# Order of work on ScalarE and VectorE in a fused four-stage kernel: when a partial sum is read, and when a masked copy is made

## Chip, cores and metric

The kernel runs on one core of a Trainium2 chip. The metric is the device time of one execution in microseconds, of which the median over several executions is given. A core has TensorE (PE, in the rows split into PE for matmuls and PEld for weight loads), VectorE (DVE), ScalarE (ACT), GpSimd (POOL) and SyncE (SP). ScalarE and SyncE also issue the DMAs of this kernel (ACTq and SPq in the rows).

## What is computed

The input x has the shape [128, 64, 1024] (batch, channel, time). Four residual stages follow one another, each over the whole tensor:

```python
x = x + L0(x, W[cond])              # per batch entry: a 64x64 mix of the channels
x = x + L1(x, K1, D1, length1)      # causal convolution along time with a kernel of 1024 taps per channel,
                                    # y * mask(t < length1)
x = x + L2(x, W2, bias, lora)       # x @ W2.T + bias + scale[adapter] * (x @ A.T) @ B.T along time
x = x + L3(x, K3, D3, length3)      # as L1, with the input masked too: y(u*mask) * mask
```

The taps are K = 2 Re(sum over n of C' exp(A dt l)). The last three stages treat each channel by itself: the convolutions mix times within a channel, and L2 has its 1024x1024 matrix along time.

## The kernel before

**Order of the whole.** First comes stage 0 (L0), with the weights and the tables of the taps prepared beside it, up to some 256 us of the span. After it a loop `body(g)` runs over 16 groups of four channels (HG = 4, NG = 16). `body(0)` is written out by itself (`early`), 1 to 13 are a hardware loop on ScalarE and VectorE, 14 has no group after the next (`more2` false), and 15 has no next group (`more1` false). Each engine has its own instruction order, written out by hand, and the engines meet at semaphores only. A pass over one group from 1 to 14 takes some 83 us.

**Precision.** Every operand of a matmul is split into two fp16 tiles, a high part (ScalarE rounds) and a low part (VectorE subtracts), and three products are summed. So ScalarE has `..._hi` helpers and VectorE `..._lo` helpers, and each low part waits for its high part.

**Stage 2 on TensorE** (`stage2`, lines 867 to 967). The 1024x1024 product is done by block products in the manner of Strassen's scheme with fewer multiplications. It is a sequence of 14 blocks, counted by `s2_summed`; here they are called block 1 to block 14. A block is 24 matmuls of line 899, and those with a low-rank part have 6 more of line 908. Blocks 1 and 2 fill the two SUM banks (PSUM 4 and 6); 3 and 4 the MIX banks (5 and 2); 5 and 6 the OWN banks (0 and 1); 7 and 8 add to the SUM banks; 9 and 10 add to the SUM banks again; 11 and 12 add to the MIX banks; 13 and 14 finish the SUM banks. Between two additions to a bank ScalarE must have copied out what stood in it at that moment, because that state is itself one of the wanted sums. This is `read_part` (line 1314; the activation is line 1320): it waits for the block (`s2_summed`), may issue a weight load (`load_w`, line 1308), reads the bank in two instructions into a tile `x3part`, and raises `s2_read`. TensorE waits for `s2_read` before the next block on that bank (line 950 for blocks 9 and 10):

```python
pe.wait_ge(s2_read, NREAD * g + 5 + p)                       # line 950, ahead of blocks 9 (p=0) and 10 (p=1)
block(SUM_AT[p], p, streamed(4), t_parts[2], False, False)
```

**The output of stage 2.** `add_part(n)` on VectorE (line 1890, instruction line 1894) adds a finished bank to its `x3part` tile once the block is done, and raises `s2_out`. `split_hi3(n)` on ScalarE (line 1327, instruction line 1333) waits for that and rounds the tile to fp16; `lo3(n)` on VectorE (instruction line 1898) makes the low part. In the same stretch the loaded channels of the next group are split: `x1_split_hi(g+1, h)` on ScalarE (line 1240, instruction line 1247) and `x1_split_lo(g+1, h)` on VectorE (instruction line 1793), four times each, in the order h = 2, 3, 0, 1. Blocks 13 and 14 wait for `s2_out` 3 and 4 (line 963), that is for `add_part(2)` and `add_part(3)`.

**Weights.** Some blocks take their weights from SBUF for good, the others from three slots that `load_w` fills from DRAM on the ACT queue. `load_w(5)` is issued in the third pair's `read_part(g, 0, ...)` and serves block 10, `load_w(6)` in `read_part(g, 1, ...)` serves block 11, and `load_w(7)`, after block 9, serves block 12.

**The end of a pass.** After stage 2 TensorE runs the states and convolution 1 of the next group (`states`, `near1`, `far1`) between those of convolution 3 of this group (`near3`, instruction line 987, and `far3`, line 1000). VectorE takes convolution 1 over into x by `take_conv1(g+1, h)`, a predicated copy under the mask (line 1795, instruction line 1800), which raises `c1_out`. `near3(g, 0)` waits for the third such copy and `near3(g, 1)` for the fourth (line 979, with `conv1_sums_read`). After a copy ScalarE rounds (`x2_split_hi`, instruction line 1251) and VectorE makes the low part (`x2_split_lo`, instruction line 1805).

**The past of convolution 3.** Where t is at or past the length, the output is the unchanged x. For this SyncE turns the split x by DMA transposes (`turn_x3`, instruction line 518), ScalarE scales the high part back (`past_half`, instruction line 1344), and VectorE adds the low part (`past_sum`, line 1844, instruction line 1848) and raises `past_ready`. SyncE waits for `past_ready` of rows 0 and 1 before it loads a table (line 473) and turns rows 2 and 3, since there are only two buffers. `take_row` (instruction line 1855) puts the past under the mask into the output.

**GpSimd** makes the tables of the taps (`make_tables`, lines 602 to 632) twice in a pass, and VectorE slows down while it runs.

Of the kernel before, what the change touches and what calls it, by code (L numbers as in the profile page):

```python
# [75 lines left out]
def build(nc, x, ids0, len1, ids2, len3, w0, ssm1, ssm3, w2, bias2, lora_a, lora_b, lora_s, out):  # L76
    with ExitStack() as ctx:
# [250 lines left out]
        SUM_AT, MIX_AT, OWN_AT = (4, 6), (5, 2), (0, 1)  # L328
# [32 lines left out]
        X1_ORDER = (2, 3, 0, 1)  # L361
# [718 lines left out]
        def _(act):  # L1080
# [159 lines left out]
            def x1_split_hi(g, h):  # L1240
                if isinstance(g, int) and g == 0:
                    act.wait_ge(x1_kept, NBLK)
                    act.wait_ge(x1_kept_last, 1)
                else:
                    act.wait_ge(x1_loaded[h], 32 * g)
                    at_least(act, out_stored[h // 2], 16 * (g - 1))
                nc.scalar.activation(x1_parts(g)[0][:, h], x1f[:, h], ACT.Copy, scale=XS / FS).then_inc(x1_hi, 1)  # L1247
# [66 lines left out]
            def read_part(g, p, bank, n_sum, row, slot, load=None):  # L1314
                act.wait_ge(s2_summed, NSUM * g + n_sum + p + 1)
                if load is not None:
                    load_w(load)
                for n in range(2):
                    o = row + 2 * p + n
                    e = nc.scalar.activation(x3part[slot + p][:, n * HW:(n + 1) * HW], ps[:, bank, n * HW:(n + 1) * HW], ACT.Identity,  # L1320
                                             bias=biasx[:, o:o + 1], scale=XS / FS)
                e.then_inc(s2_read, 1)
# [4 lines left out]
            def split_hi3(g, n, h0, row, slot):  # L1327

                if n < 6:
                    act.wait_ge(s2_out, NOUT * g + n + 1)  # L1330
                else:
                    act.wait_ge(s2_read, NREAD * g + n + 1)
                nc.scalar.activation(x3_quarter(x3h, h0, row), x3part[slot].rearrange("p (k h b) -> p k h b", k=2, h=2),  # L1333
                                     ACT.Copy).then_inc(x3_hi, 1)
# [28 lines left out]
            def body(g, more1, more2):  # L1363
                early = isinstance(g, int) and g == 0
                if more1 and not early:
                    bases_hi(0, g + 1)
                    table_hi(0, g + 1)
                act.wait_ge(low_scaled, g + 1)
                nc.scalar.activation(lowh.rearrange("p (h b) -> p h b", h=HG), lowf, ACT.Copy).then_inc(low_hi, 1)
                for h in range(HG):  # L1370
                    at_least(act, x3_turned[h], 32 * g)
                at_least(act, x3_lo, NBLK * g)
                if more1 and not early:
                    act.wait_ge(u_lo, made(0, g + 1) + 1)
                for p in range(2):
                    read_part(g, p, SUM_AT[p], 0, 0, 0)
                at_least(act, past_ready, HG * g)
                read_part(g, 0, MIX_AT[0], 2, NQ, 2, 3)
                read_part(g, 1, MIX_AT[1], 2, NQ, 2, 4)
                if early:  # L1380
                    store_tab(NBLK - 1, 1)
                act.wait_ge(low_diff, g + 1)
                nc.scalar.activation(lowdh, lowf.rearrange("p h b -> p (h b)")[:, 0:HW], ACT.Copy).then_inc(lowd_hi, 1)
                if more1:
                    for h in X1_ORDER[0:2]:
                        x1_split_hi(g + 1, h)
                if early:
                    act.wait_ge(tab_stored[1], 16 * NBLK // 2)
                split_hi3(g, 0, 0, 0, 0)
                if more1:  # L1390
                    for h in X1_ORDER[2:4]:
                        x1_split_hi(g + 1, h)
                read_part(g, 0, SUM_AT[0], 6, 0, 4, 5)
                split_hi3(g, 1, 0, 2, 1)
                read_part(g, 1, SUM_AT[1], 6, 0, 4, 6)
                if early:
                    scale_k(NBLK - 1, 3)
                    bases_hi(0, 1)
                    table_hi(0, 1)
                act.wait_ge(s2_summed, NSUM * g + 9)  # L1400
                load_w(7)
                split_hi3(g, 2, 2, NQ, 2)
                if early:
                    store_k(NBLK - 1)
                act.wait_ge(s2_summed, NSUM * g + 10)
                if more1:
                    load_w(2)
                split_hi3(g, 3, 2, NQ + 2, 3)
                act.wait_ge(s2_summed, NSUM * g + 11)
                if more1:  # L1410
                    load_w(0)
                split_hi3(g, 4, 2, 0, 4)
                bases_hi(1, g)
                act.wait_ge(s2_summed, NSUM * g + 12)
                if more1:
                    load_w(1)
                split_hi3(g, 5, 2, 2, 5)
                read_part(g, 0, 4, 12, NQ, 0)
                split_hi3(g, 6, 0, NQ, 0)
                read_part(g, 1, 6, 12, NQ, 0)  # L1420
                split_hi3(g, 7, 0, NQ + 2, 1)
                if not more1:
                    table_hi(1, g)
                if more1:
                    state_hi(0, g + 1, 0)
                    table_hi(1, g)
                    state_hi(0, g + 1, 1)
                    state_hi(1, g, 0)
                    state_hi(0, g + 1, 2)
                    state_hi(1, g, 1)  # L1430
                    past_half(g, 0)
                    state_hi(1, g, 2)
                    past_half(g, 1)
                    for h in range(HG):
                        x2_split_hi(g + 1, h)
                else:
                    for k in range(NCH - 1):
                        state_hi(1, g, k)
                for n in range(HG):
                    h = out_row(g, n)  # L1440
                    act.wait_ge(c3_summed, HG * g + n + 1)
                    at_least(act, out_stored[h], 16 * g)
                    nc.scalar.activation(outt[:, h].rearrange("p (m c) -> p m c", m=NCH),
                                         ps[:, 2 * (n % 2):2 * (n % 2) + 2, :].rearrange("p n (q c) -> p (n q) c", q=2)[:, :, ::-1],
                                         ACT.Copy, scale=1.0 / FS).then_inc(c3_out, 1)
                    if more2 and n == 1:
                        act.wait_ge(v_made, 2 * made(0, g + 2) + 2)
                    if more1 and n in (1, 2):
                        t_split_hi(g + 1, n - 1)
                        past_half(g, n + 1)  # L1450
                if more1:
                    for n in range(2, 4):
                        t_split_hi(g + 1, n)
# [11 lines left out]
        def _(dve):  # L1465
# [337 lines left out]
            def x2_split_lo(g, h):  # L1803
                dve.wait_ge(x2_hi, HG * g + h + 1)
                stt(x2l[:, h], x1f[:, h], XS / FS, x2h[:, h], ALU.mult, ALU.subtract).then_inc(x2_lo, 1)  # L1805
# [38 lines left out]
            def past_sum(g, h):  # L1844

                dve.wait_ge(past_hi, HG * g + h + 1)
                past_row = past[:, h % 2].rearrange("p (k t) -> p k t", k=NBLK)
                stt(past_row, x3t[:, h % 2, 1], 1.0 / XS, past_row, ALU.mult, ALU.add).then_inc(past_ready, 1)  # L1848
# [15 lines left out]
            def body(g, more1, more2):  # L1864

                early = isinstance(g, int) and g == 0
# [64 lines left out]
                if more1:  # L1931
                    state_lo(0, g + 1, 0)
                    table_lo(1, g)
                    state_lo(0, g + 1, 1)
                    state_lo(1, g, 0)
                    state_lo(0, g + 1, 2)
                    state_lo(1, g, 1)
                    take_conv1(g + 1, 0)
                    state_lo(1, g, 2)
                    take_conv1(g + 1, 1)  # L1940
                    past_sum(g, 0)
                    x2_split_lo(g + 1, 0)
                    take_conv1(g + 1, 2)
                    past_sum(g, 1)
                    x2_split_lo(g + 1, 1)
                    take_conv1(g + 1, 3)
                    x2_split_lo(g + 1, 2)
                    x2_split_lo(g + 1, 3)
                    t_rows(g + 1)
                else:  # L1950
                    for k in range(NCH - 1):
                        state_lo(1, g, k)
# [51 lines left out]
```

## Time and profile before

| What | Value |
|---|---|
| median of 3 runs | 1604.87 us (1602.5 to 1608.54) |
| the profiled execution, its own time | 1609.9 us |
| its span, first to last instruction | 1608.1 us |
| mean granted TensorE clock | 0.978 |
| TensorE matmul busy | 1508.5 us, 94% |
| VectorE busy | 1246.4 us, 78% |
| ScalarE busy | 743.8 us, 46% |
| GpSimd busy | 546.5 us, 34% |

The profiled execution lies 5.0 us above the median of the runs. A row of the timeline reads: start in us, duration in us, engine, line, operation, output<-inputs, shape, count; in brackets the idle time of the engine just before and what ended it. Matmuls overlap: one of 256 columns is shown with 273 ns, while the next starts 109 ns after it, so the distance of two starts tells more than a duration.

### The profile page before, as it was taken

The numbers are of one execution on the slowest core, as the hardware profiler recorded it, in microseconds if no ns is written. First come the engines' busy times: TensorE is split into PE (matmuls) and PEld (weight loads), VectorE is DVE, ScalarE is ACT, GpSimd is POOL, SyncE is SP. The second block draws the span as 40 slices with busy tenths as digits, with TensorE's granted clock in tenths as the row PEclk, the third lists the DMA queues.
The fourth block names the chain that finished last, engine by engine and source line by source line (L and its number), as shares of the span: only waits on it lengthen the run. The fifth ranks groups of instructions, "written<-read, shape, count | busy, mean of one in ns | idle before, by whom it ended". The sixth has DMA issues, their size and how long they took to land.

```text
span 1608.1 us, 36825 instructions
## 1 busy us (share of the span) xinstructions
PE 1508.5 (94%) x14983; PEld 1305.9 (81%) x14983; DVE 1246.4 (78%) x1525; ACT 743.8 (46%) x1084; POOL 546.5 (34%) x260
## 2 busy tenths in 40 slices
PE   7787776989999999999999999999999999999998
PEld 6677775778888888888888888888888888888887
DVE  7878786979595969696878787887878686969563
ACT  4444443435454535354545454545444454545443
POOL 2111103473333333333333334343434343434030
PEclk9889889999999999999999999999999999999999
DMA  7799996558575765658574757483848484857432
GB/s 225 259 323 377 339 370 223 131 119 196 131 187 139 172 153 153 173 129 192 126 191 121 193 119 204 107 219 89 225 95 214 90 229 96 223 104 210 111 132 67
DMA packets 455255, 287.63 MB, mean 179 GB/s; under 512 B 331528, under 2 KB 410896, under 8 KB 453072
## 3 DMA queue, kind: packets, MB, share of 16 engines
q1 hardware_dynamic: 405904, 174.57, 46.5%
q10 hardware_dynamic: 49216, 110.98, 19.8%
q8 instruction: 119, 1.95, 0.5%
q14 instruction: 16, 0.13, 0.0%
HBM read 161.30 MB, written 75.96 MB: 148 GB/s over the span
## 4 chain that ended last, share of the span: by engine, by line
PE 66%; DVE 19%; DMA 6%; issue 5%; ACT 3%; ACTq 0%; SPq 0%; DVEq 0%
PE ps L899 27%; PE ps L803 8%; PE ps L987 6%; DMA arena<-in_x_dram 5%; PE ps L876 5%; PE ps L908 4%; PE ps L847 4%; PE ps L751 3%; DVE arena L1793 3%; PE ps L1000 3%; PE ps L813 3%; DVE arena L1848 3%; DVE arena L1805 2%; DVE lowd L1885 2%; PE ps L687 1%
## 5 line engine op out<-in xcount | busy, mean ns | idle before, releaser
L899 PE MATMUL ps<-arena,w2t 128*128 128x256 f16 x4608 | 525.4, 273 | 17.2 <-ACT arena L1320 14.0
L899 PEld LDWEIGHTS ps<-arena,w2t 128*128 128x128 f16 x4608 | 450.1, 98 | 77.5 <-issue 17.6
L618 POOL TENSOR_TENSOR arena<-arena 128x1024 f32<-128x1024 f32 x31 | 78.3, 2525 | 796.7 <-DVE arena L1855 430.2
L1898 DVE TENSOR_TENSOR arena<-arena 128x512 f16<-128x512 f32 x128 | 104.3, 815 | 126.0 <-ACT arena L1333 126.0
L1333 ACT ACTIVATE arena<-arena 128x512 f16<-128x512 f32 x128 | 80.6, 630 | 253.7 <-DVE arena L1894 252.7
L751 PE MATMUL ps<-arena 128*128 128x128 f32 x1024 | 147.7, 309 | 51.5 <-DMA arena<-in_x_dram 26.4
L751 PEld LDWEIGHTS ps<-arena 128*128 128x128 f32 x1024 | 139.7, 221 | 57.0 <-DMA arena<-in_x_dram 28.1
L1320 ACT ACTIVATE arena<-ps,biasx 128x256 f32<-128x256 f32 x256 | 103.3, 470 | 85.5 <-PE ps L908 51.3
L847 PE MATMUL ps<-arena 128*128 128x512 f16 (+1 forms) x768 | 136.9, 329 | 5.6 <-DVE arena L1793 5.6
L987 PE MATMUL ps<-arena 128*128 128x256 f16 (+1 forms) x1536 | 137.1, 246 | 2.6 <-DVE gbuf L1800 2.6
L987 PEld LDWEIGHTS ps<-arena 128*128 128x128 f16 x1536 | 122.0, 98 | 16.5 <-DVE gbuf L1800 6.3
L1793 DVE SCALAR_TENSOR_TENSOR arena<-gbuf,arena 128x1024 f16<-128x1024 f32 x64 | 129.1, 2037 | 0.5 <-ACT arena L1247 0.5
L847 PEld LDWEIGHTS ps<-arena 128*128 128x128 f16 x768 | 74.4, 99 | 56.0 <-issue 7.7
L1251 ACT ACTIVATE arena<-gbuf 128x1024 f16<-128x1024 f32 x64 | 67.5, 1055 | 86.2 <-DVE gbuf L1800 84.6
L1782 DVE SCALAR_TENSOR_TENSOR arena<-ps,arena 128x512 f16<-128x512 f32 x48 | 33.2, 692 | 79.7 <-ACT arena L1290 79.7
L899 PE MATMUL ps<-arena,gbuf 128*128 128x256 f16 x768 | 89.1, 273 | 0.0
L628 POOL TENSOR_TENSOR arena<-arena 128x1024 f32<-128x1024 f32 x31 | 86.8, 2799 | 2.4
L876 PE MATMUL ps<-arena,at 128*128 128x512 f16 x384 | 85.5, 379 | 0.0
L1800 DVE COPY_PREDICATED gbuf<-mask,ps 128x1024 f32<-128x1024 uint8 x64 | 83.4, 1304 | 1.3 <-issue 1.3
L1894 DVE SCALAR_TENSOR_TENSOR arena<-ps,arena 128x512 f32<-128x512 f32 x96 | 65.6, 684 | 23.8 <-PE ps L908 23.4
L899 PEld LDWEIGHTS ps<-arena,gbuf 128*128 128x128 f16 x768 | 75.1, 98 | 8.7
L1344 ACT ACTIVATE arena<-arena 128x1024 f32<-128x1024 f16 x60 | 63.0, 1050 | 40.5 <-DVE arena L1855 40.5
(253 smaller groups left out, 2718.4 us busy)
## 6 DMA issues: line engine op xcount, KB each, us to landing
w2t<-w_scratch ACTq DMA_DIRECT2D x96, 512.0 KB, 3.9
arena<-in_x_dram SPq DMA_DIRECT2D x64, 512.0 KB, 8.1
out_dram<-arena SPq DMA_DIRECT2D x64, 512.0 KB, 3.4
gbuf<-x_scratch SPq DMA_DIRECT2D x120, 256.0 KB, 4.3
gbuf<-w_scratch ACTq DMA_DIRECT2D x32, 512.0 KB, 3.9
arena<-krow_scratch SPq DMA_DIRECT2D x31, 512.0 KB, 9.3
x_scratch<-arena ACTq DMA_DIRECT2D x14, 1024.0 KB, 10.7
x_scratch<-arena ACTq DMA_DIRECT2D x14, 896.0 KB, 7.7
```

The source lines that it names most:

```text
L628: ptt(v4, v4, m4, ALU.add).then_inc(v_made, 1)
L751: mm = nc.tensor.matmul(ps[:, s, j * P:(j + 1) * P], xin[:, l % NXIN, j, odd * P:(odd + 1) * P], pick[:, l * GPAIRS + j, :], start=True, s ...
L803: mm = nc.tensor.matmul(o, ut[v][:, part, 2 * h + blk, :], xx[:, h, 2 * k + blk, :], start=(h == 0 and q == 0 and blk == 0), stop=(k == 0 ...
L847: nc.tensor.matmul(o, g1[:, h, part, d * P:(d + 1) * P], m, start=(d == 0 and q == 0), stop=False)
L876: mm = nc.tensor.matmul(ps[:, 7, :], at[:, part, k, :], xx[:, :, k, :], start=(k == 0 and q == 0), stop=(k == NBLK - 1 and q == 2))
L899: mm = nc.tensor.matmul(ps[:, bank, n * HW:(n + 1) * HW], weight(p, n, part, k), xx[:, :, k, :], start=(fresh and n == 0 and k == 0 and q ...
L987: nc.tensor.matmul(ps[:, bank, c0:c0 + w], xx[:, h, j, :], g3[:, h, part, g0:g0 + w], start=(j % 4 == 0 and xx is x3h and part == 0), stop ...
L1320: e = nc.scalar.activation(x3part[slot + p][:, n * HW:(n + 1) * HW], ps[:, bank, n * HW:(n + 1) * HW], ACT.Identity, bias=biasx[:, o:o + 1 ...
L1333: nc.scalar.activation(x3_quarter(x3h, h0, row), x3part[slot].rearrange("p (k h b) -> p k h b", k=2, h=2), ACT.Copy).then_inc(x3_hi, 1)
L1793: stt(lo[:, h], x1f[:, h], XS / FS, hi[:, h], ALU.mult, ALU.subtract).then_inc(x1_lo, 1)
L1800: nc.vector.copy_predicated(x1f[:, h].rearrange("p k b -> p (k b)"), mask1[:, :, :].rearrange("p k b -> p (k b)"), ps[:, b0:b0 + 2, :].rea ...
L1898: tt(x3_quarter(x3l, h0, row), x3part[slot].rearrange("p (k h b) -> p k h b", k=2, h=2), x3_quarter(x3h, h0, row), ALU.subtract).then_inc( ...
```

## The change

On ScalarE, in `body(g)`: the read of SUM bank 0 after block 7 goes ahead of `split_hi3(0)` (except in group 0, where `split_hi3(0)` keeps its place), and ahead of the last two rounding steps of x1. The read of bank 1 after block 8 goes ahead of `split_hi3(1)`. The two x1 steps now stand one after `split_hi3(0)` and one after `split_hi3(1)`. In group 15 there are no x1 steps, and only reads and splits change places. The weight loads 5 and 6 move with their reads. On VectorE, in the tail of `body(g)` for groups 0 to 14: `past_sum(0)` goes behind `take_conv1(g+1, 2)`, and `past_sum(1)` behind `take_conv1(g+1, 3)`. No instruction is added or removed, and no wait is changed.

```diff
@@ ScalarE, body(g, more1, more2) @@
                 if early:
                     act.wait_ge(tab_stored[1], 16 * NBLK // 2)
-                split_hi3(g, 0, 0, 0, 0)
+                if early:
+                    split_hi3(g, 0, 0, 0, 0)
+                read_part(g, 0, SUM_AT[0], 6, 0, 4, 5)
+                if not early:
+                    split_hi3(g, 0, 0, 0, 0)
                 if more1:
-                    for h in X1_ORDER[2:4]:
-                        x1_split_hi(g + 1, h)
-                read_part(g, 0, SUM_AT[0], 6, 0, 4, 5)
+                    x1_split_hi(g + 1, X1_ORDER[2])
+                read_part(g, 1, SUM_AT[1], 6, 0, 4, 6)
                 split_hi3(g, 1, 0, 2, 1)
-                read_part(g, 1, SUM_AT[1], 6, 0, 4, 6)
+                if more1:
+                    x1_split_hi(g + 1, X1_ORDER[3])
                 if early:
                     scale_k(NBLK - 1, 3)
                     bases_hi(0, 1)
@@ VectorE, body(g, more1, more2) @@
                     state_lo(1, g, 2)
                     take_conv1(g + 1, 1)
-                    past_sum(g, 0)
                     x2_split_lo(g + 1, 0)
                     take_conv1(g + 1, 2)
-                    past_sum(g, 1)
+                    past_sum(g, 0)
                     x2_split_lo(g + 1, 1)
                     take_conv1(g + 1, 3)
+                    past_sum(g, 1)
                     x2_split_lo(g + 1, 2)
                     x2_split_lo(g + 1, 3)
                     t_rows(g + 1)
```

## Rows read from the trace of the kernel before

**Rows 1.** The page's first part: busy time and share of the span.

```profile
PE 1508.5 (94%) x14983; PEld 1305.9 (81%) x14983; DVE 1246.4 (78%) x1525; ACT 743.8 (46%) x1084; POOL 546.5 (34%) x260
```

**Rows 2.** Waits of TensorE: us in total, times, longest.

```profile
PE ps L899 <- ACT arena L1320: 14.0, 15, 2.5
...
PE ps L803 <- ACT arena L1320: 4.0, 1, 4.0
PE ps L987 <- DVE gbuf L1800: 2.6, 15, 0.3
```

**Rows 3.** Windows, one pass: length, busy by engine, PEclk, DMA share, GB/s.

```profile
877.00:960.00 83.00, 82.00 (x831) 69.87 (x829) 65.12 (x66) 40.02 (x57) 31.93 (x14) 1.00 0.66 158
```

**Rows 4.** Timeline of one middle group, blocks 8 and 9.

```profile
896.48 0.68 DVE L1894 SCALAR_TENSOR_TENSOR arena<-ps,arena 128x512 f32<-128x512 f32 x1
896.96 2.78 PE L899 MATMUL ps<-arena,w2t 128*128 128x256 f16 x24
...
897.19 0.63 ACT L1333 ACTIVATE arena<-arena 128x512 f16<-128x512 f32 x1 [5.59 <-DVE arena L1894]
897.43 0.34 ACTq L1308 DMA_DIRECT2D gbuf<-w_scratch  x1
897.73 1.99 ACT L1247 ACTIVATE arena<-gbuf 128x1024 f16<-128x1024 f32 x2
...
899.62 0.81 ACT L1320 ACTIVATE arena<-ps,biasx 128x256 f32<-128x256 f32 x2
...
900.58 2.78 PE L899 MATMUL ps<-arena,w2t 128*128 128x256 f16 x24 [0.84 <-ACT arena L1320]
```

**Rows 5.** The same group after block 9.

```profile
901.84 2.35 DVE L1793 SCALAR_TENSOR_TENSOR arena<-gbuf,arena 128x1024 f16<-128x1024 f32 x2
...
910.69 0.69 DVE L1894 SCALAR_TENSOR_TENSOR arena<-ps,arena 128x512 f32<-128x512 f32 x1 [1.20 <-PE ps L908]
...
913.68 2.78 PE L899 MATMUL ps<-arena,w2t 128*128 128x256 f16 x24
```

**Rows 6.** Landing times of the weight loads, line 1308.

```profile
DMA to landing us min/median/max: 3.1/3.9/8.7
```

**Rows 7.** Timeline of the same group, masked copies and near3.

```profile
937.28 1.31 DVE L1800 COPY_PREDICATED gbuf<-mask,ps 128x1024 f32<-128x1024 uint8 x1
...
937.98 1.06 POOL L632 TENSOR_TENSOR arena<-twin,arena 128x512 f32<-128x512 f32 x1
938.50 1.63 DVE L1848 SCALAR_TENSOR_TENSOR arena<-arena 128x1024 f32<-128x1024 f16 x1
...
939.11 0.82 PE L864 MATMUL ps<-gbuf,arena 128*128 128x256 f16 x6
...
940.05 1.21 DVE L1805 SCALAR_TENSOR_TENSOR arena<-gbuf,arena 128x1024 f16<-128x1024 f32 x1
...
941.19 1.30 DVE L1800 COPY_PREDICATED gbuf<-mask,ps 128x1024 f32<-128x1024 uint8 x1
...
944.66 1.29 DVE L1800 COPY_PREDICATED gbuf<-mask,ps 128x1024 f32<-128x1024 uint8 x1
...
944.69 1.15 PE L1000 MATMUL ps<-gbuf,arena 128*128 128x256 f16 x9
...
946.00 2.15 PE L987 MATMUL ps<-arena 128*128 128x256 f16 x24 [0.17 <-DVE gbuf L1800]
```

**Rows 8.** The fourth row's past_half in this group; landing of transposes, line 518.

```profile
957.41 1.05 ACT L1344 ACTIVATE arena<-arena 128x1024 f32<-128x1024 f16 x1
```

```profile
DMA to landing us min/median/max: 3.1/3.4/5.0
```

**Rows 9.** Timeline of group 0, blocks 9 and 12.

```profile
310.99 4.22 PE L899 MATMUL ps<-arena,w2t 128*128 128x256 f16 x24 [2.50 <-ACT arena L1320]
...
319.63 1.49 ACT L1265 ACTIVATE arena<-arena 128x1536 f16<-128x1536 f32 x1 [3.86 <-POOL arena L632]
...
323.22 2.79 PE L899 MATMUL ps<-arena,w2t 128*128 128x256 f16 x24 [0.58 <-DMA w2t<-w_scratch]
```

## The prediction, made before the changed kernel had run

> **What bounds the kernel now.** I read the page's busy shares first. TensorE is busy for 94% of the span, the next engine for 78% [rows 1], so only what lets TensorE stand still can cost time once the loop runs. The windows say the same of one pass: 82.00 of 83 us busy, at the full granted clock, 1.00 [rows 3]. What is to be had in a pass is thus about one microsecond and a bit. Next I read the list of TensorE's waits, to see who holds that microsecond. Two of its lines carry the steady loop: line 899 waits for ScalarE's read of a partial sum, 15 times for 14.0 us, and line 987 waits for VectorE's masked copy, 15 times for 2.6 us [rows 2]. The change touches just these two. The third line shown, 4.0 us once, belongs to group 0. Last I read the timeline of one middle group round the two places, because a wait in the list is shorter than the time really lost: the end of a matmul is modelled, and the distance of starts is what counts.
>
> **ScalarE's part, groups 1 to 14.** Block 8 starts at 896.96 [rows 4]. Its 24 matmuls are 109 ns apart, so block 9 could start 2.62 us later, at 899.58. It starts at 900.58 [rows 4]: 1.00 us lost, where the wait shows 0.84. ScalarE explains it. It sat idle for 5.59 us until `add_part(0)` let `split_hi3(0)` go at 897.19, then ran two x1 steps from 897.73 (1.99 us), and read the bank only at 899.62 [rows 4]. Block 7, for which the read really waits, had ended before block 8 began.
>
> In the new order ScalarE is free when block 7 ends. The read runs from about 897.1 to 897.9 (0.81 us by its row), `split_hi3(0)` to 898.6, x1 step three to 899.6. The read of bank 1 must wait for the end of block 8, some 899.7, and is done at 900.5; block 10 wants it only 3.27 us (30 matmuls) after 899.58, at 902.85. So the wait ahead of block 9 goes, and none comes ahead of block 10. Gain 1.00 us in each of 14 groups, 14.0 us.
>
> The DMAs move with it. Load 5 is issued at 897.43 now, as the ACT queue runs ahead of the engine [rows 4], and will be issued at about 897.2. With the median landing of 3.9 us [rows 6] it is there at 901.1, and block 10 starts at 902.85: 1.7 us to spare. Load 6 comes earlier than now, as it no longer stands behind `split_hi3(1)`, and load 7 is issued when block 9 is done, as before. The longest landing of 8.7 us [rows 6] can't be the rule here, since the trace of before shows no such wait in the loop.
>
> What gets later: the fourth x1 step stands behind `split_hi3(1)`, which waits for `add_part(1)`. VectorE's two low parts at 901.84 follow right on that sum [rows 5], so the split goes at about 901.95 and x1 step four ends near 903.65 instead of 899.7. VectorE makes the two low parts in a row, 2.35 us; the second must now wait some 0.7 us, so `add_part(2)` slips by 0.8 us, to about 906.2 done. The first who wants it is block 13, at 913.68 now [rows 5] and 912.7 or less then: 6 us to spare. VectorE idles 1.20 us before `add_part(4)` at 910.69 [rows 5], and by `add_part(5)` the slip is used up. I cost it at nothing; it is covered by TensorE's blocks 10 to 12, and if this cover were gone it would cost 0.8 us a group.
>
> **ScalarE's part, groups 0 and 15.** In group 0 the same wait is 2.50 us [rows 9], and the read would come 2 us earlier, as two x1 steps leave the queue ahead of it. But block 12 then waits for load 7, which ScalarE issues only after a rounding step that stood waiting 3.86 us for GpSimd until 319.63 [rows 9], and GpSimd's chain isn't touched. A lead won at block 9 is given back there. I take 0, with 0 and 2.5 us as ends. After the wait the row shows 4.22 us for 24 matmuls against 2.78 [rows 4, 9]: there the clock was at its lower level, 1.2 GHz. The Trainium skill, page "TensorE: Matmul & The Clock Gate", Part 1, says that idle time drops the array to half its rate and that sustained work restores it. By it a shorter wait in group 0 might save the slow stretch too, some 1.4 us more by these rows; the other way, a longer wait ahead of block 12 might put a slow stretch there. Either would again be taken up by the chain of group 0. In group 15 the reads only change places with two splits, and no wait stands there (of the 15 waits one is group 0's): 0.
>
> **VectorE's part.** `near3(1)` waits for the fourth masked copy. `far3(0)` starts at 944.69, its 9 matmuls take 0.98 us, and `near3(1)` could start at 945.67; it starts at 946.00 [rows 7], 0.33 lost, where the list shows 0.17. From 937.28 on VectorE is busy without a pause: copy 2, past sum, low part, copy 3, past sum, low part, copy 4 [rows 7]. Each past sum ahead of a copy delays it. In the new order the low part of row 0 follows copy 2 at 938.5. I give it the 1.63 us that the past sum took there beside GpSimd [rows 7], and not the 1.21 of a quiet one: copy 3 can start at 940.1. Its data are there after `far1(2)`, which starts at 939.11 and takes 0.82 us [rows 7], 939.93, so VectorE doesn't wait. Copy 3 ends at 941.4, the first past sum (1.2) at 942.6, a low part at 943.8, copy 4 at 945.1. That is 0.6 us ahead of 945.67. The wait goes: 15 times 0.33 us, 5.0 us. What the whole stretch issues stays the same, so the work behind it (the differences for the next stage 2) ends at the same time as now.
>
> Two past sums get later, from 940.1 to 942.6 and from 943.6 to 946.2. Behind each stands the SP queue, with a table load and two transposes. The second pair then starts near 946.6 and 947.9 and lands by 953 even with the longest landing of 5.0 us [rows 8]; `past_half(3)` wants it at 957.41 [rows 8]. 4.5 us remain. Cost 0.
>
> **Sum.** 14.0 + 5.0 = 19.0 us. The profiled execution took 1609.9 us, which gives 1590.9. It lies 5.0 us above the median of 1604.87; against that median the forecast is 1585.9, a gain of 1.2%.
>
> **The rivals.**
>
> *Only ScalarE's part pays.* The margin of the fourth copy is 0.6 us, and VectorE shares memory access with GpSimd: while GpSimd's line 632 runs from 937.98 for 1.06 us, the past sum beside it takes 0.42 us longer than a quiet low part [rows 7]. If the low part now in that place and the copy behind it both stretch by more than that, the wait for the copy stays. The page "SBUF — State Buffer" of the Trainium skill, in its terms, says of the port pair of these two engines that the loser "fully blocks"; by that alone the low part would start when line 632 ends, 939.04, copy 4 would end at 945.2, and the wait would still go. Time: 1604.9 - 14.0 = 1590.9. Chance 0.13.
>
> *The wait moves on inside stage 2.* The stall at block 9 was where TensorE met the late VectorE chain once a pass. Without it TensorE comes 1.33 us earlier to all that follows, and the later `add_part(2)` or a weight load could hold block 10, 11 or 13. Against it: margins of 1.7 us (load 5) and 6 us (block 13). If half of the 19.0 us came back so: 1595.4. Chance 0.07.
>
> *Group 0 gains too*, because the chain from its block 9 on is more TensorE's than I think, by up to 2.5 us plus the slow stretch of 1.4: 1582 to 1585. Chance 0.10.
>
> *Slower.* The past sums come so late that the SP queue's transposes of rows 2 and 3 hold `past_half(3)`; behind it in ScalarE's order stand the last output row and two splits that the next stage 2 needs. It decides once the second past sum slips by more than the 2.6 us worked out and the 4.5 of margin together, 7.1. If it slipped by 9.1 us, and every microsecond past the margin went to TensorE, that is 2.0 us in 15 groups, 30 us, less the gain: 1604.9 - 19.0 + 30 = 1615.9. Chance 0.03.
>
> *The change does nothing*, as another signal already sets both starts at these times. Against it: both waits name just the instruction that moves. 1604.9. Chance 0.04.
>
> **How the numbers follow.** The forecast has the remaining 0.63, its own spread some 3 us, from the runs of before (1602.5 to 1608.54). A measurement of this kernel tells about 0.5% (8 us) from no change. Faster by more than that, below 1596.9: forecast, first and third rival, and nearly all of the second, 0.92, from which I take 0.04 for what I haven't seen, so 0.88. Same: the last rival and most of what I took off, 0.08. Slower: the fourth and a rest, 0.04. The range goes from group 0 gaining with a quick set of runs, 1581, to ScalarE's part alone with a slow one, 1595.
>
> **What would show each step.** Right: in a middle group block 9 starts 2.62 us after block 8, the list has no more line 899 <- line 1320 save one in group 0, and a pass is 1.33 us shorter. `near3(1)` starts 0.98 us after `far3(0)`. VectorE idles before the second of its last two x1 low parts. Wrong: a new releaser of about 1 us at line 899 (a DMA, or line 1894), line 987 still waiting for line 1800, group 0 longer or shorter by over 1 us, or line 1344 waiting for a DMA.

## The result and the profile after

The changed kernel took 1588.23 us (median of 4 runs, 1587.08 to 1591.55) against 1605.14 us before (4 runs). The ratio is 0.9897, with a 95% interval of 0.9873 to 0.9921: 1.0% faster. The forecast was 1585.9 us. Beside e1 and e2 the changed kernel was measured once more (6 runs against 17 of the kernel before): 1587.14 against 1607.45 us, ratio 0.9878 (0.9856 to 0.99).

The diff lengthens the file by four lines ahead of VectorE's part, so VectorE's line 1800 is now 1804, 1848 is 1852, 1894 is 1898, and so on; lines up to 1385 keep their numbers. The edits of some experiments shift them again: the instruction of `add_part` is line 1895 in e3 and line 1899 in e7 and e8. These are TensorE's waits at lines 899 and 803 for DMAs and for ScalarE in the changed kernel, in the form of [rows 2]: us in total, times, longest.

```profile
PE ps L899 <- DMA w2t<-w_scratch: 4.2, 1, 4.2
PE ps L803 <- ACT arena L1320: 4.0, 1, 4.0
...
PE ps L899 <- ACT arena L1320: 0.6, 1, 0.6
```

Both lines of the steady loop are gone: line 899 waits for line 1320 once, 0.6 us, in group 0, and line 987 waits for nothing. What is left of these is group 0's, and the longest of line 899 is now one for a weight load, which was 0.58 us before [rows 9]. The window of one pass shows the same, in the form of [rows 3]:

```profile
877.00:958.00 81.00, 81.00 (x827) 69.54 (x825) 64.26 (x66) 39.50 (x56) 31.47 (x15) 1.00 0.65 162
```

TensorE is busy for 81.00 of 81 us, against 82.00 of 83 before; the distance from one pass to the next is 81.43 us, where it was 82.75. The timeline of the same place as [rows 4], blocks 7 to 10 of a middle group:

```profile
882.42 2.78 PE L899 MATMUL ps<-arena,gbuf 128*128 128x256 f16 x24
884.78 0.68 DVE L1898 SCALAR_TENSOR_TENSOR arena<-ps,arena 128x512 f32<-128x512 f32 x1
...
885.04 5.40 PE L899 MATMUL ps<-arena,w2t 128*128 128x256 f16 x48
885.24 0.34 ACTq L1308 DMA_DIRECT2D gbuf<-w_scratch  x1
...
885.63 0.84 ACT L1320 ACTIVATE arena<-ps,biasx 128x256 f32<-128x256 f32 x2 [5.95 <-PE ps L899]
886.36 0.63 ACT L1333 ACTIVATE arena<-arena 128x512 f16<-128x512 f32 x1
886.88 1.05 ACT L1247 ACTIVATE arena<-gbuf 128x1024 f16<-128x1024 f32 x1
...
888.44 0.84 ACT L1320 ACTIVATE arena<-ps,biasx 128x256 f32<-128x256 f32 x2 [0.51 <-issue]
...
890.93 2.78 PE L899 MATMUL ps<-arena,gbuf 128*128 128x256 f16 x24
...
891.87 1.23 DVE L1797 SCALAR_TENSOR_TENSOR arena<-gbuf,arena 128x1024 f16<-128x1024 f32 x1 [0.51 <-ACT arena L1247]
```

Blocks 8 and 9 are one row now, 48 matmuls without a gap. ScalarE waits for TensorE ahead of the read, no longer for VectorE. The read of bank 1 is over at 889.28, 1.65 us before block 10. VectorE idles 0.51 us ahead of its last x1 low part, which is the price that the prediction put at 0.7 us and covered.

The other place, in the form of [rows 7]:

```profile
924.37 1.32 DVE L1804 COPY_PREDICATED gbuf<-mask,ps 128x1024 f32<-128x1024 uint8 x1
...
925.64 1.57 DVE L1809 SCALAR_TENSOR_TENSOR arena<-gbuf,arena 128x1024 f16<-128x1024 f32 x1
...
927.14 1.29 DVE L1804 COPY_PREDICATED gbuf<-mask,ps 128x1024 f32<-128x1024 uint8 x1
...
930.61 1.29 DVE L1804 COPY_PREDICATED gbuf<-mask,ps 128x1024 f32<-128x1024 uint8 x1
...
931.77 1.15 PE L1000 MATMUL ps<-gbuf,arena 128*128 128x256 f16 x9
...
932.75 2.14 PE L987 MATMUL ps<-arena 128*128 128x256 f16 x24
```

The fourth copy ends at 931.90, and `near3(1)` starts at 932.75, 0.98 us after `far3(0)`. The low part beside GpSimd took 1.57 us, where a quiet one takes 1.21 [rows 7].

**Where the time went.** The timelines can be cut at fixed points of TensorE's order: the start of block 1 of group 0, the start of line 876 (the low-rank products) in groups 1 and 15, and the end of the span. The 14 passes between the two starts of line 876 hold all of the steady loop. All in us, from the profiled execution of each kernel:

| Kernel | start of block 1 | group 0 | 14 passes | from there to the end |
|---|---|---|---|---|
| before | 279.98 | 95.64 | 1158.15 | 74.33 |
| changed | 276.17 | 95.46 | 1140.02 | 74.35 |
| changed, again | 276.39 | 94.81 | 1140.02 | 74.4 |
| e1, ScalarE's part alone | 279.81 | 95.93 | 1144.67 | 74.3 |
| e2, VectorE's part alone | 277.27 | 95.62 | 1157.01 | 74.3 |
| e3, read behind the split | 283.11 | 95.80 | 1141.11 | 74.4 |
| e4, x1 steps together | 278.71 | 94.91 | 1140.02 | 74.4 |
| e5, only the second past sum moved | 277.43 | 95.77 | 1140.02 | 74.4 |
| e6, past sums far later | 283.00 | 95.87 | 1145.85 | 74.3 |
| e7, load 7 early in group 0 | 274.92 | 94.80 | 1140.11 | 74.4 |
| e8, e7 and bases later | 275.04 | 94.11 | 1140.07 | 74.3 |

The gain lies in the 14 passes: 18.13 us, or 1.30 us a pass (1.32 in all but the last). The start of block 1 scatters by 8 us over these executions, from 274.92 to 283.11, though nothing ahead of it differs between the kernels. That is most of the scatter of the measured times, and the reason why the passes are compared here rather than whole spans.

### The profile page after: what moved, and what is told of

Its sections match the earlier page's. It is cut to its first block, busy times and chain, and to the rows that moved or that the text cites. A ratio compares the mean times of both kernels' runs of the same rounds, so it can differ in the third digit from the quotient of the medians.

```text
span 1586.0 us, 36825 instructions
## 1 busy us (share of the span) xinstructions
PE 1503.4 (95%) x14983; PEld 1307.5 (82%) x14983; DVE 1241.6 (78%) x1525; ACT 744.8 (47%) x1084; POOL 545.5 (34%) x260
## 3 DMA queue, kind: packets, MB, share of 16 engines
q10 hardware_dynamic: 49216, 110.98, 20.3%
## 4 chain that ended last, share of the span: by engine, by line
PE 84%; DVE 8%; DMA 6%; issue 1%; ACT 1%; SPq 0%; DVEq 0%; ACTq 0%
PE ps L899 35%; PE ps L803 8%; PE ps L987 8%; PE ps L847 8%; DMA arena<-in_x_dram 5%; PE ps L908 5%; PE ps L876 5%; PE ps L1000 4%; PE ps L751 3%; PE ps L813 3%; PE ps L864 2%; PE ps L860 1%; PE ps L687 1%; DVE arena L1692 1%; DVE arena L1797 1%
## 5 line engine op out<-in xcount | busy, mean ns | idle before, releaser
L1447 ACT ACTIVATE arena<-ps 128x1024 f32<-128x1024 f32 x64 | 65.0, 1017 | 36.0 <-PE ps L1000 35.9
```

## The experiments

All diffs are against the changed kernel, except those of e1 and e2, which are halves of the change. e3 to e8 were measured once each (1596.17, 1589.77, 1589.35, 1600.84, 1585.96 and 1585.34 us), so only their profiles are compared, by the table above.

**e1: ScalarE's part alone.** The first half of the change's diff, with VectorE's order as before.

> ScalarE's part alone, VectorE's order as before. Theory A (as predicted, the two parts add up): 14.0 us less than before, some 1591, no wait at block 9 in groups 1 to 14, the wait of near3(1) for the fourth masked copy still 0.33 us per pass by the distance of starts, a pass of 81.75 us. Rival B (the two waits are one chain of VectorE, so that only both parts together free TensorE): less than 11 us gained, and a wait for line 1894 or a low part grows at line 899.

Measured: ratio 0.9916 (0.9897 to 0.9935), 13.8 us less at the medians (1593.61 against 1607.45). The 14 passes took 13.48 us less than before. TensorE's list:

```profile
PE ps L987 <- DVE gbuf L1804: 2.4, 13, 0.2
```

Theory A holds: the block 9 wait is gone, and the wait of `near3(1)` is left as it was, 13 times 0.18 us by the list. These 13 passes take 81.79 us each, and the last of the 14, which has no such wait, 81.43. VectorE's part on top of this is worth another 4.65 us in the 14 passes.

**e2: VectorE's part alone.** The second half of the diff, with ScalarE's order as before.

> VectorE's part alone, ScalarE's order as before. Theory A (the parts add up): 5.0 us less than before, some 1600, a pass of 82.42 us. Theory B (the chain of before runs on VectorE from the masked copies through all later work to add_part(0), which lets split_hi3(0), two x1 steps and the read go): the wait of near3(1) goes, but the read comes no earlier, so the wait at block 9 grows from 1.00 to 1.33 us, the pass stays 82.75 us and the time stays at 1605.

Measured: ratio 0.9994 (0.998 to 1.0009), no difference. The 14 passes took 1.14 us less than before, where a sum of two independent parts would have it 4.65. TensorE's waits:

```profile
PE ps L899 <- ACT arena L1320: 17.6, 16, 2.5
```

The `near3(1)` wait is gone, but this line has grown from 14.0 to 17.6 us [rows 2]; 0.3 us of that is a second wait in group 0, and the rest is block 9 of the loop, 1.06 us a pass where it was 0.82. In a middle group it is this:

```profile
897.38 2.78 PE L899 MATMUL ps<-arena,w2t 128*128 128x256 f16 x24 [1.05 <-ACT arena L1320]
```

1.05 us against 0.84 [rows 4]. So theory B is right in the main: the fourth copy comes earlier, but the VectorE work behind it does not, and that work ends in `add_part(0)`, which let the read go in the old order. TensorE only waited later.

The profile of the kernel before shows this chain as a closed ring. From 936.67, where TensorE and then ScalarE let VectorE go on to copies 2 to 4, to the next `add_part(0)` at 979.23 it is 42.56 us, in which VectorE has only one pause over 0.2 us (0.70, a round trip through ScalarE). From `add_part(0)` to block 9 it is 4.10 us (896.48 to 900.58), and from block 9 to where VectorE starts again 36.09 (to 936.67). The three add up to 82.75, the pass. In e2 the same three stretches are 42.46, 4.10 and 36.09 us, 82.65 together, and that is its pass. So the order of the copies alone takes nothing out of the ring but 0.1 us.

**e3: the read behind split_hi3(0).** Only the x1 steps are moved behind the read.

```diff
-                if early:
-                    split_hi3(g, 0, 0, 0, 0)
-                read_part(g, 0, SUM_AT[0], 6, 0, 4, 5)
-                if not early:
-                    split_hi3(g, 0, 0, 0, 0)
+                split_hi3(g, 0, 0, 0, 0)
+                read_part(g, 0, SUM_AT[0], 6, 0, 4, 5)
```

> The changed kernel, but split_hi3(0) stays ahead of the read in all groups; only the x1 steps stand behind it. Theory A (the two x1 steps were what held the read): in a middle group add_part(0) ends some 2.9 us after block 7 starts, the split and the read take 1.5 us more, which is 0.7 us ahead of the time block 9 can start. No wait, a pass of 81.42 us as in the changed kernel. Rival B (the read must not wait for VectorE's add_part(0) at all): a wait at block 9 comes back, 0.3 us or more per pass.

Measured: a pass is 81.43 us in all but two of the 14, which together are 1.1 us longer, with one wait of 0.8 us for load 5. In a middle group ScalarE splits at 892.92 as soon as `add_part(0)` allows, and reads right after:

```profile
892.92 0.63 ACT L1333 ACTIVATE arena<-arena 128x512 f16<-128x512 f32 x1 [5.81 <-DVE arena L1895]
...
893.46 0.82 ACT L1320 ACTIVATE arena<-ps,biasx 128x256 f32<-128x256 f32 x2
```

The read is over at 894.28. Blocks 8 and 9 are one row from 892.47, so block 9 starts at 895.09: 0.8 us of margin. Theory A holds; it was the two x1 steps that made the read late. Putting the read ahead of the split adds margin, but gains no time in a normal pass. Load 5, which is issued with the read, is issued 5.36 us ahead of block 10 in this kernel and 5.69 us in the changed one. In the pass with the wait block 10 started 6.27 us after the issue, so the earlier issue would have shortened that wait by 0.3 us and not prevented it. That is an estimate from these distances.

**e4: both x1 steps together.**

```diff
                 if more1:
-                    x1_split_hi(g + 1, X1_ORDER[2])
+                    for h in X1_ORDER[2:4]:
+                        x1_split_hi(g + 1, h)
                 read_part(g, 1, SUM_AT[1], 6, 0, 4, 6)
                 split_hi3(g, 1, 0, 2, 1)
-                if more1:
-                    x1_split_hi(g + 1, X1_ORDER[3])
```

> The changed kernel, but both x1 steps stand between split_hi3(0) and the read of bank 1. Theory: the read of bank 1 ends about 1.1 us ahead of block 10, so TensorE doesn't wait, and VectorE's 0.51 us idle before its fourth x1 low part goes; a pass of 81.42 us, no difference in time. If the splitting of the x1 pair matters, a wait for line 1320 at block 10 shows.

Measured: 1140.02 us for the 14 passes, the same to a hundredth. In a middle group the read of bank 1 is over 1.33 us ahead of block 10, and VectorE's idle 0.51 us is gone. That the pair was split is worth nothing in time.

**e5: past_sum(0) back in its old place.**

```diff
                     take_conv1(g + 1, 1)
+                    past_sum(g, 0)
                     x2_split_lo(g + 1, 0)
                     take_conv1(g + 1, 2)
-                    past_sum(g, 0)
                     x2_split_lo(g + 1, 1)
                     take_conv1(g + 1, 3)
                     past_sum(g, 1)
```

> The changed kernel, but past_sum(0) stands where it stood before (ahead of the third masked copy); only past_sum(1) is behind the fourth. Theory A (the order of the first past sum is nothing, since near3(0) had its copy in time in groups 1 to 13): a pass of 81.42 us, only group 0 loses some 0.4 us at near3(0). Rival B (the lead of copy 3 is what makes copy 4 early): near3(1) waits again for the masked copy, 0.1 us or more per pass.

Measured: 1140.02 us again. The third copy, after which the change is named, does nothing for the time in the passes; what counts is that one past sum less stands ahead of the fourth. In its group 0 the list of waits has no line 987, so the 0.4 us expected there didn't show.

**e6: the past sums far later.**

```diff
                     take_conv1(g + 1, 2)
-                    past_sum(g, 0)
                     x2_split_lo(g + 1, 1)
                     take_conv1(g + 1, 3)
-                    past_sum(g, 1)
                     x2_split_lo(g + 1, 2)
                     x2_split_lo(g + 1, 3)
+                    past_sum(g, 0)
                     t_rows(g + 1)
+                    past_sum(g, 1)
```

> The changed kernel with the past sums far later: the first ahead of t_rows, the second behind it, so that the second ends some 10 us later than in the changed kernel instead of the 2.5 by which that one moved it. By the margin worked out in the prediction (4.5 us beyond the change at past_half(3)) past_half(3) now waits for the transposes, about 5 us, and the last row's output and the last two splits slip. A slower rival would need this to reach TensorE: if all of it does, a pass is 2 to 5 us longer, 30 us or more in all; if the next stage's slack before blocks 3 to 9 (some 6 us) takes it up, a pass stays at 81.42 us.

Measured: 1145.85 us for the 14 passes, 5.83 more. But a pass is 81.43 us in ten of them; the other four are longer by 4.88, 0.49, 0.38 and 0.08 us. In a middle group `past_half(3)` waits, though for 0.93 us and not for 5:

```profile
954.64 1.06 ACT L1344 ACTIVATE arena<-arena 128x1024 f32<-128x1024 f16 x1 [3.83 <-DVE arena L1859]
...
958.48 1.06 ACT L1344 ACTIVATE arena<-arena 128x1024 f32<-128x1024 f16 x1 [0.93 <-DMA arena<-arena]
```

Against TensorE's line 876 the second past sum ends 7.7 us later than in the changed kernel here, not 10 (10.4 later than before). And the row ahead of `past_half(3)` was 0.5 us late itself, as its copy into the output stands behind the second past sum on VectorE. In this group TensorE notices none of it. In all groups `past_half(3)` waits, 0.63 to 2.20 us. The longest of these waits does reach TensorE on the path of the slower rival: at 1204.13 `past_half(3)` had waited 2.20 us, VectorE's past sum at 1205.22 waited for it (1.52 us), and at 1214.67 TensorE waited 0.22 us for VectorE's line 1878. That pass is the one that is 0.38 us longer.

The pass with 4.88 us goes another way:

```profile
566.87 0.34 ACTq L1308 DMA_DIRECT2D gbuf<-w_scratch  x1
...
575.66 4.46 PE L899 MATMUL ps<-arena,gbuf 128*128 128x256 f16 x24 [2.93 <-DMA gbuf<-w_scratch]
```

Load 5 was issued right after block 7, and block 10 started only 8.8 us later, against 5.7 us in the changed kernel (885.24 to 890.93). In that pass the transposes of line 488 on the SP queue were issued late, at 565.31, 1.56 us ahead of load 5. In the changed kernel's pass above they were issued at 880.74, 4.5 us ahead of it. So it may be that late past sums push the SP queue's transfers into load 5, whose margin was worked out as 1.7 us. That isn't shown. For it: over the 14 passes of e6 the transposes lead load 5 by 1.56 to 5.18 us, in the changed kernel by 3.66 to 6.36, and the slow pass has the shortest lead. Against it: another pass of e6 had a lead of 1.80 us and no wait for the load, and the one wait for load 5 in e3 came with a lead of 5.13 us.

**e7 and e8: group 0.** e7 moves one load, and e8 adds a move on VectorE.

```diff
                 if early:
                     scale_k(NBLK - 1, 3)
                     bases_hi(0, 1)
-                    table_hi(0, 1)
                 act.wait_ge(s2_summed, NSUM * g + 9)
                 load_w(7)
+                if early:
+                    table_hi(0, 1)
```

```diff
-                bases_lo(1, g)
+                if not early:
+                    bases_lo(1, g)
                 add_part(5, 2, 5)
                 lo3(5, 2, 2, 5)
+                if early:
+                    bases_lo(1, g)
```

> The changed kernel; in group 0 alone weight load 7 is issued ahead of the table rounding that waits for GpSimd. Theory A (as predicted, group 0's end is set by GpSimd's and VectorE's chain): the 4.16 us wait at block 12 goes, TensorE waits the longer at block 14 or at line 803 for line 1320, and the distance from the first block of group 0 to that line's start stays 62.1 us. Rival B (the weight load is on the path): it shrinks by up to 4 us.

> As e7, and in group 0 VectorE makes the low part of the next bases (3.36 us beside GpSimd) behind add_part(5) and its low part instead of ahead. If VectorE's chain ends group 0, then add_part(5), the read and TensorE's start at line 803 come some 3.3 us earlier: 58.8 us from the first block instead of 62.1, and the time is 3 to 4 us below the changed kernel. If GpSimd alone sets it, nothing changes.

Measured in e7: the wait for the load at block 12 is gone, and TensorE waits at the next block, 13, for `add_part(2)` instead. The second row is line 803 at the end of group 0's stage 2.

```profile
321.23 4.15 PE L899 MATMUL ps<-arena,w2t 128*128 128x256 f16 x24 [3.94 <-DVE arena L1899]
...
336.99 2.11 PE L803 MATMUL ps<-arena 128*128 128x128 f16 x24 [4.02 <-ACT arena L1320]
```

From the first block at 274.92 to line 803 it is 62.07 us, as in the changed kernel (276.17 to 338.25, 62.08) and before (279.98 to 342.05, 62.07). Theory A holds to a hundredth: what is won inside group 0 without touching VectorE's chain is given back.

Measured in e8: line 803 starts 58.77 us after block 1, as was expected of VectorE's chain. But the low part of the bases that moved is also what the transposes of line 488 wait for, and so TensorE waits a little on:

```profile
333.81 1.51 PE L803 MATMUL ps<-arena 128*128 128x128 f16 x24 [0.72 <-ACT arena L1320]
...
341.33 1.51 PE L803 MATMUL ps<-arena,gbuf 128*128 128x128 f16 x24 [1.50 <-DMA gbuf<-arena]
```

Of the 3.3 us, 0.7 is left at the end of group 0 (94.11 against 94.80 in e7). From block 1 to the end of the span e8 took 1308.5 us, the changed kernel 1309.8 and 1309.2. That is less than the times scatter by, so e8 is no proven improvement on the changed kernel.

## Why the prediction was right, and where not

**The sum.** Forecast 19.0 us, of which 18.3 stand in group 0 and the 14 passes of the profile (95.64 + 1158.15 against 95.46 + 1140.02). The medians gave 16.9 and, measured again, 20.3. That they lie on both sides of 18.3 fits the scatter of the start of block 1, but the runs without a profile don't show where that start was.

**ScalarE's part, 14.0 us:** right. e1 shows 13.48 us in the passes. Each step of it came: the read right after block 7, load 5 issued with it (885.24), 0.51 us of idle time at the x1 low part where 0.7 was worked out, and `add_part(2)` with no wait behind it.

**VectorE's part, 5.0 us:** right as a term on top of the other, with 4.65 in the passes, 13 times 0.36; the other two of the 15 waits were both group 0's. But the prediction added the two parts as if each held for itself, and e2 shows that they don't. The chain that made the read late ran on VectorE from the masked copies to `add_part(0)`. The page's chain that ended last had it at 19% VectorE before, and has it at 8% after. The prediction read the idle 5.59 us of ScalarE up to `add_part(0)` [rows 4], but didn't draw from it that time won ahead of that point on TensorE alone is lost again. That the sum came out all the same is because both parts were made together. Its first rival, with only ScalarE's part paying, doubted the right term for a reason that didn't come: beside GpSimd the low part took 0.36 us longer, and the fourth copy still ended 0.85 us ahead of `near3(1)`. What the prediction had no rival for is that VectorE's part can't pay alone.

**Which moves count.** The step "copy 3 can start at 940.1" was right and of no use. By e5, e4 and e3 three of the moves, each taken back by itself, change nothing in a normal pass: the first past sum, the split of the x1 pair, and the read ahead of `split_hi3(0)`. The gain thus hangs on the x1 steps behind the read and the second past sum behind the fourth copy. The read of bank 1 ahead of `split_hi3(1)` was never taken back by itself, and the three not all together, so that these two moves would be enough is argued and not shown.

**Group 0, taken at 0 us for ScalarE's part:** right up to line 803, 62.07 and 62.08 us from block 1. Block 12 started 43.24 us after block 1 before and 43.27 after, as load 7 set it. The wait at block 9 shrank by 1.9 us and that at block 12 grew from 0.58 to 4.16, partly because the slow stretch behind block 9 was gone. Behind the longer wait there now came a slow stretch, as the prediction had left open:

```profile
319.44 4.35 PE L899 MATMUL ps<-arena,w2t 128*128 128x256 f16 x24 [4.16 <-DMA w2t<-w_scratch]
...
338.25 2.74 PE L803 MATMUL ps<-arena 128*128 128x128 f16 x24 [3.97 <-ACT arena L1320]
```

24 matmuls of the first form take 2.78 us elsewhere, and the 24 of line 803 take 1.50. At this place line 803's took 2.04 before, and 2.74 here. So what VectorE's part gives at the end of group 0, where `near3(0)` and `near3(1)` both waited before (0.22 and 0.25 us by the list), came out as 0.2 us (95.64 to 95.46), and as 0.8 in the second profile, where line 803 took 2.12.

**The slower rival:** its place was right, its price wrong. It let every microsecond beyond the margin go to TensorE in each pass. e6 put the second past sum 10.4 us later than before, beyond the 7.1 at which the rival was to decide, and ten of the 14 passes stayed as they were. `past_half(3)` waited in each, but only the longest of these waits, 2.20 us, is seen to reach TensorE, as 0.38 us. Most of what e6 cost, 4.88 us, was a late load 5 in one pass.

## What to carry to other kernels

Two waits of the bounding engine are not two terms until it is known that they don't hang on one chain of another engine; follow that chain from the first wait to the second before adding, and see whether its pieces add up to the pass. Where an engine that works in order holds a short instruction that the bounding engine waits for, put that instruction ahead of those that have time. When a first group differs from the loop, compare from fixed points of the bounding engine's order: here that took away a scatter of 8 us and left hundredths in the passes.

## What wasn't expected of the hardware

A wait costs more than its length when the clock falls behind it, and the same wait doesn't always do it. In e6 a wait of 2.93 us lengthened its pass by 4.88 us, as the next 24 matmuls took 4.46 instead of 2.78 us; the granted clock was 0.59 while they ran (575.7 to 579.9). Before, the 2.50 us wait of group 0 was followed by 24 matmuls in 4.22 us [rows 9], at a granted clock of 0.64 (311 to 315), and of 0.50, the lower level (1.2 GHz), from 313 to 315. In e2 the same place had this row:

```profile
308.29 2.78 PE L899 MATMUL ps<-arena,w2t 128*128 128x256 f16 x24 [2.52 <-ACT arena L1320]
```

The wait is as long, and there is no slow stretch: the granted clock was 1.00 from 308.3 to 310.9. In the windows shown the 1 us waits of the loop had none: the granted clock of the pass was 1.00 before and after. A term for the clock in a forecast is thus better put as a chance than added to the sum.
